# Taking the skip term D*x of a state-space mixer off TensorE, and unrolling its loops

## The reference

```python
zxbcdt = jnp.einsum('bld,ed->ble', x, in_proj_w)      # z, xBC and dt
xBC = silu(conv(xBC_t) + conv_b)                      # 4 taps, one filter for each channel
x_ssm, Bm, Cm = xBC[..., :256], xBC[..., 256:384], xBC[..., 384:]
# state-space scan: h = h * exp(dt * A) + dt * x * B;  y = h . C
y = ys + D[None, None, :, None] * x_ssm               # the skip term
y = y * silu(z)
y = y * rsqrt(mean(y * y) + EPS) * norm_w             # 256 channels
y = einsum('bld,ed->ble', y, out_proj_w) + x          # then a layer norm
```

## Time and profile before

| | |
|---|---|
| median of 3 runs | 396.58 us |
| the profiled execution, its time and its span | 397.04 us, 395.1 us |
| PE, DVE, ACT, POOL busy, share of the span | 84%, 66%, 50%, 48% |
| first mixture of experts, up to about | 123 us |
| mixer, from its first taps to its last projection | about 146 to 253 us |
| last mixture of experts, from about | 272 us |

### The profile page before, as it was taken

One profiled execution on the slowest core, in us unless ns is written; L12 is line 12 of the kernel. 1 busy time (PEld: TensorE's weight loads), 2 busy tenths in 40 slices (PEclk: granted clock), 3 DMA queues, 4 the chain that ended last, 5 costly groups with the idle time before them and its releaser, 6 DMA issues.

```text
span 395.1 us, 9001 instructions
## 1 busy us (share of the span) xinstructions
PE 331.0 (84%) x2386; PEld 297.8 (75%) x2386; DVE 262.3 (66%) x939; ACT 196.6 (50%) x473; POOL 187.7 (48%) x217
## 2 busy tenths in 40 slices
PE   7868999999960788999999998695689999999800
PEld 7758999999950763677767776695679999999700
DVE  4696666555434999486777769899966666554326
ACT  3712666667732135439374662146026666777420
POOL 4005777776552031764717453020057777774611
PEclk9997999999985775899999999696669999999955
DMA  6693455555425000000000000002034555554363
GB/s 164 229 314 117 163 189 185 190 182 189 170 101 213 1 2 0 0 0 2 0 2 0 0 1 2 0 2 80 27 102 142 187 188 184 188 189 168 120 226 106
DMA packets 29904, 42.70 MB, mean 108 GB/s; under 512 B 5362, under 2 KB 14756, under 8 KB 29860
## 3 DMA queue, kind: packets, MB, share of 16 engines
q1 hardware_dynamic: 24900, 31.67, 23.1%
q0 software_dynamic: 4096, 8.40, 7.4%
q10 hardware_dynamic: 864, 2.11, 1.3%
HBM read 14.33 MB, written 7.34 MB: 55 GB/s over the span
## 4 chain that ended last, share of the span: by engine, by line
PE 61%; DVE 25%; DMA 5%; issue 4%; POOL 2%; ACT 2%; DVEq 0%; SPq 0%; ACTq 0%
PE PS L671 17%; PE PS L683 16%; DVE X L1312 4%; PE PS L720 4%; PE PS L727 3%; PE PS L774 3%; PE PS L554 3%; DVE stats L1143 3%; DMA YT_all<-y_rows 2%; POOL y_rows L473 2%; DVE onehot_b L1232 2%; DVE XT_all L1457 2%; PE PS L656 2%; PE PS L564 2%; PE PS L846 2%
## 5 line engine op out<-in xcount | busy, mean ns | idle before, releaser
L465 POOL DMA_INDIRECT XG<-xn_rows,rows_in x64 | 60.7, 949 | 74.7 <-DVE rows_in L1241 28.6
L671 PE MATMUL PS<-XT_all,W1B 128*128 x624 | 83.6, 277 | 2.0 <-DVE XT_all L1271 2.0
L683 PE MATMUL PS<-H,W2B 128*128 128x128 f32 x624 | 82.6, 276 | 0.0
L671 PEld LDWEIGHTS PS<-XT_all,W1B 128*128 128x128 f32 x624 | 75.9, 192 | 3.3 <-issue 3.0
L683 PEld LDWEIGHTS PS<-H,W2B 128*128 128x128 f32 x624 | 75.8, 192 | 0.3
L473 POOL DMA_INDIRECT y_rows<-YS,rows_out x64 | 61.4, 959 | 30.2 <-issue 15.2
L959 ACT ACTIVATE H<-PS,W1B 128x128 f32<-128x128 f32 x156 | 48.8, 364 | 43.6 <-PE PS L671 41.5
L1292 DVE TENSOR_SCALAR YT_all<-PS,W2B 128x128 f32 x78 | 27.4, 352 | 63.5 <-PE PS L683 63.5
L949 ACT ACTIVATE W1B<-W1S 128x516 f32 x78 | 49.4, 633 | 35.4 <-DVE te_i L1250 25.9
L554 PE MATMUL PS<-ones 128*128 128x128 f32 x256 | 44.7, 355 | 16.4 <-DVEq L1597 15.3
L554 PEld LDWEIGHTS PS<-ones 128*128 128x128 f32 x256 | 43.5, 269 | 16.6 <-DVEq L1597 15.5
(11 more groups left out here) (194 smaller groups left out, 506.4 us busy)
## 6 DMA issues: line engine op xcount, KB each, us to landing
W2B<-W2S SPq DMA_DIRECT2D x78, 256.5 KB
W1S<-in_L_ffn_W SPq DMA_DIRECT2D x1, 2048.0 KB, 8.5
W2S<-in_L_ffn_W SPq DMA_DIRECT2D x8, 256.0 KB, 6.8
xn_rows<-XN SPq DMA_DIRECT2D x8, 256.0 KB, 3.2
YT_all<-y_rows SPq DMA_DIRECT2D x4, 512.0 KB, 6.0
YT_all<-y_rows ACTq DMA_DIRECT2D x4, 512.0 KB, 6.3
X<-in_L_attn_x SPq DMA_DIRECT2D x4, 256.0 KB, 4.9
XG<-xn_rows,rows_in POOLq DMA_INDIRECT x64
```

Of the source, the lines that this page charges most:

```text
L465: g.indirect_dma_start(out=XG[:, u, :], out_offset=None, in_=xn_dram, in_offset=bass.IndirectOffsetOnAxis(ap=rows_in[:, i:i + 1], axis=0)) ...
L671: last = mm(PS[2 + 2 * half + j % 2][:, c * P:(c + 1) * P], W1B[w][:, h * P:(h + 1) * P], XT_all[:, ds(start, P)], start=True, stop=True)
L683: last = mm(PS[1 + 6 * (j % 2)][:, 0:P], W2B[w][:, c * D:(c + 1) * D], H[w][:, c, :], start=(c == 0), stop=(c == HC - 1))
```

## The change

The diagonal matrix and the two matmuls with it are gone. ACT makes `skip` = D * `conv` for the whole of the next batch, two instructions of 128x512, after the squares of the batch's last chunk. DVE adds `skip` to the transposed output in PS[7] and writes `skipped`; a second instruction multiplies that with the gate into `y2T`. The second waits for the first, and PE, ACT and POOL wait for the second, as they did for the single one. The hardware loops of all four engines are written out.

```diff
-                        for i in range(IC):
-                            mm(PS[6][:, i * P:(i + 1) * P], conv[i][:, tile], diagD[:, i, :], start=(i == 0),
-                               stop=False, skip_group_check=True)
                         pe.wait_ge(s_mix, q + 1)
                         pe.wait_ge(s_xd, q + 1)
                         for h in range(HEADS):
                             last = mm(PS[6][:, h * HD:(h + 1) * HD], mix[u][:, h, :], xdt[u][:, h * HD:(h + 1) * HD],
-                                      start=False, stop=True, skip_group_check=True)
+                                      start=True, stop=True, skip_group_check=True)
...
                         if beyond(n, 1):
                             act.wait_ge(s_yp, n * NC)
+                            act.wait_ge(s_skip, n)
+                            if m == 0:
+                                act.wait_ge(s_act, st.n)
                         A(conv[BLOCKS[m]][:], acc[m][:], ACT.Silu).then_inc(s_silu, 1)
...
                     squares(NC - 1)
-
+                    if not last_batch:
+                        skips(b + 1)
+
+                def skips(b):
+                    if b:
+                        act.wait_ge(s_skipped, b * NC)
+                    act.wait_ge(s_silu, b * 6 + TAPS)
+                    for i in range(IC):
+                        last = A(skip[:, i, :], conv[i], ACT.Copy, scale=Dch[:, i:i + 1])
+                        if i < IC - 1:
+                            st.done(last)
+                    last.then_inc(s_skip, 1)
...
                 load_table(ACT.Exp)
-                batch(0)
-                with act.Fori(1, BATCH - 1) as b:
-                    batch(b)
-                batch(BATCH - 1, True)
+                skips(0)
+                for b in range(BATCH):
+                    batch(b, b == BATCH - 1)
...
-                        v.tensor_tensor(y2T[:, c, :, :], PS[7][:, 0:INNER].rearrange("p (i t) -> p i t", i=IC),
+                        dve.wait_ge(s_skip, b + 1)
+                        v.tensor_tensor(skipped[c % 2][:], PS[7][:, 0:INNER].rearrange("p (i t) -> p i t", i=IC),
+                                        skip[:, :, c * P:(c + 1) * P], ALU.add).then_inc(s_skipped, 1)
+                        dve.wait_ge(s_skipped, q + 1)
+                        v.tensor_tensor(y2T[:, c, :, :], skipped[c % 2][:],
                                         gz[:, :, ds(q, 1), :].rearrange("p i a t -> p i (a t)"), ALU.mult).then_inc(s_y2, 1)
```

More of the change, by code:

```diff
@@ L47, in __init__ @@
     def __init__(self, engine, sem):
-        self.engine, self.sem, self.base, self.n, self.fixed = engine, sem, 0, 0, 0
+        self.engine, self.sem, self.n = engine, sem, 0
     def done(self, instruction):
@@ L54, in settle @@
     def settle(self):
-        self.engine.wait_ge(self.sem, self.base + self.n)
+        self.engine.wait_ge(self.sem, self.n)
     def link(self, instruction):
@@ L60, in link @@
         self.settle()
[L62 to L69, removed]
 BLOCKS = (2, 3, 0, 1, 4, 5)
@@ L144, in macaron_block @@
         nw = sb("nw", [P, IC])
-        diagD = sb("diagD", [P, IC, P])
+        skip = sb("skip", [P, IC, SEQ])
+        skipped = [sb(f"skipped{u}", [P, IC, P]) for u in range(2)]
         lnw = sb("lnw", [P, D])
@@ L332, in macaron_block @@
         s_lnb = sem("s_lnb")
+        s_skip = sem("s_skip")
+        s_skipped = sem("s_skipped")
         block = ctx.enter_context(nc.Block())
@@ L529, in batch @@
                             g.tensor_tensor(heads(S_kept[:]), heads(S[:]), by_chunk(2, q), ALU.mult).then_inc(s_kept, 1)
-                batch(0)
-                with pool.Fori(1, BATCH - 1) as b:
-                    batch(b)
-                batch(BATCH - 1, True)
+                for b in range(BATCH):
+                    batch(b, b == BATCH - 1)
                 for q in range(NT - 3, NT):
@@ L1172, in parameters @@
                 dve.wait_ge(s_w1s, 1)
-                for c in range(IC):
-                    st.done(v.tensor_scalar(diagD[:, c, :], ident[:], Dch[:, c:c + 1], None, ALU.mult))
-                st.settle()
             def logits(layer, part, lo, hi):
```

## The result

The changed kernel took 402.2 us (median of 4 runs, 400.8 to 405.1) beside 397.0 for the kernel before (4 runs): ratio 1.0134, 95% interval 1.0090 to 1.0178, so 3.6 to 7.1 us slower. The forecast was 400.8, slower. The profiled execution took 400.8 us with a span of 399.0, 3.9 more than before.

The account below looks back on a forecast made before the run. PE was taken to bound the first three batches, with a DVE-ACT loop close behind, and DVE the last. Terms summed to +4.25 us: 401.3 profiled, 400.8 median, the forecast's own range 398.8 to 403.6, overall 396.6 to 403.8.

Parts of the forecast that it names:

- The skip of batch 0: Start of the mixer: ACT's skip delays its copy of B and decays by 1.26 us, counted as 0.05.
- unrolling: DVE before `y2T`: written-out loops remove an idle issue gap of 0.17 us, 2 x 0.17 = -0.34 in all.
- PE's pairs: Removed matmul pairs, 0.45 us each: chunk 1 gains, chunk 0's taken off the skips, chunk 2's lost waiting for S.
- ACT's skips less slack: Two instructions before ACT's copy of B, 1.26 us, less 0.28 in hand in batches 1 and 2, none in batch 3.
- DVE's second instruction: `y2T` ready 0.52 us later per chunk: +1.56 through chunk 3, +1.56 in batch 3, and +0.90 for POOL.
- a second loop just behind PE: Batch 1, DVE and ACT through `y2T`, squares, tap and S: 0.46 us in hand in a round of 5.21.
- Chunk 3: Batches 0 to 2: ACT's row to the silus and PE's next transposes move by 0.52 us, +1.56 in all.
- rival (a): PE stays the bound, DVE's and ACT's work fits beside it; 9 pairs give -4.0 us, time 394.1; chance 0.10.
- DVE beside POOL: Chunk 1: the multiply waits 0.3 us beside POOL's `seg_rhs` in each of three batches, +0.90 (0 to 3.12).
- rival (c): DVE and POOL shut each other out for whole instructions: 3.12 us in place of 0.90, time 403.0; chance 0.08.
- (b): PE's gain comes, ACT's tap isn't late, but ACT's skips cost what they must: +0.5 us, 397.1; chance 0.13.
- (d): TensorE's clock falls after PE's new waits for one batch, 5 us or more: about 406; chance 0.05.

Follow-up runs that it names:

- unroll_again: The kernel before with its four hardware loops written out, nothing else, run a second time: ratio 0.9970 to the kernel before.
- unroll: The kernel before with its four hardware loops written out, nothing else, first run: ratio 0.9953 to the kernel before.
- noskip: The changed kernel without any skip term: no skip instructions on ACT, no addition on DVE, no pairs on PE; ratio 0.9892 to the kernel before.
- noadd: The changed kernel without DVE's addition, ACT still making `skip`: ratio 1.0011 to the kernel before.
- skiponce: The changed kernel with ACT making `skip` only for batch 0, DVE adding that buffer in all batches: ratio 1.0102 to the kernel before.
- reorder: The changed kernel with ACT squaring `y2T` after applying the tap in batches 0 to 2: ratio 1.0058 to the kernel before.
- both: The changed kernel with ACT's squares after the tap and its skips of batches 1 to 3 moved to chunk 1: ratio 0.9996 to the kernel before.
- mixed: The changed kernel, ACT's squares and skips moved later, last batch keeping PE's pairs and DVE's single multiply: 394.1 us beside 397.5, ratio 0.9925.

## Why the prediction was right, step by step

By stages, the forecast's terms and the trace (after less before):

| stage, us | forecast | measured |
|---|---|---|
| start and batch 0 | +0.42 | +0.75 |
| batch 1 | +0.73 | +0.86 |
| batch 2 | +0.73 | +0.67 |
| start of batch 3 and its DVE work | +2.37 | +2.11 |
| sum | +4.25 | +4.39 |

The first line holds an error that the sum hides. The skip of batch 0 was forecast at 0.05; it pushes ACT's `eseg` back, and PE waits for it:

```profile
162.67 1.10 PE L717 MATMUL PS<-seg_rhs,after 128*128 128x512 f32 x2 [1.50 <-ACT eseg L1008]
```

Before, PE came there at nearly the same time (162.66), without such a wait, after it had worked at the lower clock until 160.90. In unroll_again, where the clock was 0.79 over the first 3 us, it is 4.12 us from `la` to this place, for 4.97 after.

By terms, for one of the two middle batches, the measured ones as the differences unroll - before, noskip - unroll, noadd - noskip and after - noadd (so that each is on top of the ones ahead of it):

| term, us in a batch | forecast | measured |
|---|---|---|
| unrolling | -0.17 | -0.38 |
| PE's pairs (three of 0.45) | -1.35 | -0.86 |
| ACT's skips less slack | +0.98 | +0.79 |
| DVE's second instruction (0.45 lost in chunk 2, 0.52 in chunk 3, 0.30 for POOL) | +1.27 | +1.21 |
| sum | +0.73 | +0.76 |

With DVE's instruction put in first, it costs 1.68 and the skips 0.33 (skiponce); the last two lines are right only in this order.

*What bounds.* Right: a second loop just behind PE. With the pairs gone PE waited for S in chunk 2 (0.83, 0.28, 0.29 in batches 0 to 2), and reorder took this wait away. But the 0.46 us in hand was misread. It takes one transpose from the chain and the other, in batch 3, from a timeline, and the chain prints the same transposes 0.16 later. The timeline's row of before is

```profile
199.39 0.38 PE L802 MATMUL PS<-ident,yt 128*128 128x128 f32 x2
```

so the slack was 199.39 - 198.94 - 0.15 = 0.30. With the forecast's own 0.52 the round of chunk 2 should then have become 0.2 longer, and it did not (5.21 before and after). From the transpose to the end of `y2T` the loop grew by 0.53 (194.18 to 195.32 before, 194.79 to 196.46 after), but from the tap on DVE to S it shrank by 0.23 (196.65 to 198.53 before, 197.79 to 199.44 after), and 0.53 - 0.23 is the 0.30. I think that `yi` no longer stands behind PE's share of the state (L778, now L765), which starts 2.12 and not 2.57 us after the transpose; no run was made for that. Two errors cancelled here, which is luck.

*Chunk 3.* The forecast sent its 0.52 through the squares, the tap and the silus to PE's next start. The squares came 0.59 later after the transpose (1.07 before, 1.66 after), but what ended last was DVE's own branch of the same chain: tap, taps, `yi`, `yt`, and now two instructions to `y2T` of chunk 2, for which PE's last transpose waits.

```profile
204.82 2.17 ACT L999 ACTIVATE XT_all<-XT_all 128x512 f32<-128x512 f32 x4
...
206.49 0.43 DVE L1525 TENSOR_TENSOR y2T<-skipped,YT_all 128x256 f32<-128x256 f32 x1
```

The silus end at 206.99, 0.32 before PE's start of the next batch (207.31); `y2T` ends at 206.92, and the transpose follows at 207.06 after a wait of 0.62. The stretch grew by 0.81, not 0.52. This wait and the one for the taps (0.42) I had not named; reorder took both away as well.

*PE's pairs.* The largest error of a single term, 0.49 a batch. The pairs of chunks 1 and 2 were worth what was forecast (0.38 and 0.45 in noskip). That of chunk 0, which the forecast took off the skips' price, was worth nothing: PE waits for `mix` there, as rival (a) had it. For chunk 3's, which the forecast left out, noskip shows 0.09, since ACT's chain to the silus stood 0.16 behind PE.

*Unrolling.* Too small, -0.17 for 0.28 and 0.48 measured, and in the wrong place: the gap before `y2T` stands in a stretch that is 5.21 us long with and without the loops. That the gain was so near is luck too.

*DVE's second instruction.* Right in size, and in place but for the end of chunk 3. In the last batch 1.56 was forecast; from S to the transpose it is 18.00 us (235.62 to 253.62) in place of 16.72 (232.87 to 249.59), +1.28, because the addition starts 0.44 to 0.46 before the multiply and not 0.52. The rest of the last stage's +2.11 is 0.66 before this S, for 0.81 forecast, and 0.17 behind the transpose, where nothing was forecast.

*ACT's skips.* The price was right, 1.22 for the two and 1.26 forecast, and so was the place in batches 1 to 3: waits for btok of 0.95, 0.96 and 1.82. But taken away by themselves they give back only 0.33 in a middle batch (after - skiponce), because `mix` is nearly as late as btok. A sum of terms hides that.

The total came within 0.14 us of the trace with errors of 0.2 to 0.5 in the terms, which cancel. That closeness is luck; the sign, the size of some 4 us and most of the places are not.

*DVE beside POOL.* The multiply took 0.61 and 0.62 in chunk 1, beside `seg_rhs`, and 0.42 elsewhere, 0.20 for 0.30 forecast; POOL after:

```profile
195.15 1.04 POOL L481 TENSOR_TENSOR seg_rhs<-upto,la 128x512 f32<-128x512 f32 x1
```

It ended at 196.19 and the multiply, begun at 195.85, at 196.46, 0.27 later. The pair of the earlier trace rows taken singly, before:

```profile
258.44 1.43 POOL L543 TENSOR_TENSOR X<-X,YT_all 128x512 f32<-128x512 f32 x1 [6.75 <-ACT YT_all L1105]
...
258.66 1.36 DVE L1373 SCALAR_TENSOR_TENSOR X<-YT_all,rs,X 128x128 f32<-128x128 f32 x1
```

POOL ends at 259.87 and this DVE instruction, 0.34 long elsewhere in these rows, at 260.02, 0.15 later. In both places DVE ends after POOL by less than its own length, 0.15 us less in one and 0.19 in the other: as if it were held until POOL is done, but with its first 0.15 to 0.19 us already behind it. So rival (c)'s mechanism fits, and its sign, a multiply of more than 0.6 us, was there; its price of 1.04 each was not, since POOL had only 0.34 us to go. The Trainium skill ("SBUF — State Buffer", section "Who interferes with whom") has the rule that the later of the two is blocked until the first has ended; the two pairs of rows agree with it, but for that first part. No run here moved the multiply against `seg_rhs`.

*The rivals.* (a) fell: PE's busy time went down by 6.5 us in the first window, and the mixer grew. (b) fell too: it needed ACT's tap on time, and DVE's wait for the tap grew from 0.36 to 0.79; that both comes out at 0.9996, with the chains moved away, is another mechanism with (b)'s number. (d) was seen in single executions, at 2.5 us and not 5; in the median it isn't shown. Its sign, a granted clock below 0.95 from 160 to 250 us, was absent in the profile after (1.00).

The median rose by 5.3 us (3.6 to 7.1 by the ratio) to 402.2, 1.4 above the forecast, the mixer's trace by 4.39. The rest is inside the interval.

## What to carry to other kernels

Before work is moved off a full engine, follow the loop of the next engines around once and write down how much it has in hand in a round: here 0.30 us, against 0.45 that the change could give, and a dependent instruction of 0.44 was put into that very loop. Take both ends of such a difference from the same view of the profile. Where an engine waits for a result and has independent work standing behind that wait, changing their order was worth more (1.0 us a batch) than moving the new work away (0.33). And a change can be right for one stage only: with the skip term on ACT and DVE in the batches where PE is full, on PE in the one where DVE is, and ACT's order mended, the kernel was 0.75% faster than before, 0.3 to 0.5% of which the written-out loops give by themselves.

## What was not expected of the hardware

An idle time of 1.82 us on PE was followed by the lower of its two clock levels in one execution (L761 1.81 us) and not in another (1.01 us) of the same code. In seven profiled executions PE waited 1.71 to 1.74 us for S in the last batch (1.73 in after), and the transpose behind it took 0.41 each time, the upper level. A wait of 3.32 us was followed by a transpose of 0.66 in before and of 0.41 in mixed, where the clock fell 0.9 us later (granted clock 0.50 from 247.44 on). So the length of the wait alone does not decide in these traces.

The hardware loops cost 0.28 and 0.48 us in a pass of 22.4 written out, all in the first stretch of the pass; the issue gap of 0.17 on DVE that the profile shows lies elsewhere and lengthened nothing.

A multiply with both sources in SBUF took 0.2 us longer beside a GpSimd instruction that ended 0.34 us after its start.
